# A convolution and a focused linear attention over 16 images: where the last state product, the norms, the high half of O and the floor stand, and inner loops written out

## What is computed

```python
x = x + _L0_conv_ref(_gn(x), ...)   # 3x3 grouped convolution, 8 groups of 32; kernels rotated by an
                                    # angle that a small MLP finds per image; output scaled per channel
x = x + _L1_conv_ref(_gn(x), ...)   # focused linear attention, 8 heads of 32:
#   q, k = relu(x Wq + bq) + 1e-6, relu(x Wk + bk) + 1e-6, both divided by softplus(scale)
#   q = q**3 * |q| / |q**3| ; k likewise            (norms over all 256 channels of a token)
#   z = 1 / (q . sum_tokens(k) + 1e-6) ; state = sum_tokens(k^T v) ; out = (q @ state) * z
#   out = out + depthwise 5x5 convolution of v ;  out = out @ Wproj + bproj
```

## Time and profile before

| | before |
|---|---|
| median of 3 runs (lowest to highest) | 3786.84 us (3786.37 to 3790.71) |
| the profiled execution: its own time | 3783.43 us |
| its span | 3781.6 us |
| PE busy, share of the span | 3485.4 us, 92% |
| DVE, ACT, POOL busy | 73%, 70%, 42% |
| mean granted TensorE clock | 0.989 |

### The profile page before, as it was taken

One profiled execution on the slowest core, in us unless ns is written; L12 is line 12 of the kernel. 1 busy time (PEld: TensorE's weight loads), 2 busy tenths in 40 slices (PEclk: granted clock), 3 DMA queues, 4 the chain that ended last, 5 costly groups with the idle time before them and its releaser, 6 DMA issues.

```text
span 3781.6 us, 84370 instructions
## 1 busy us (share of the span) xinstructions
PE 3485.4 (92%) x27988; PEld 2840.5 (75%) x27988; DVE 2762.7 (73%) x6715; ACT 2658.7 (70%) x7096; POOL 1606.0 (42%) x1557
## 2 busy tenths in 40 slices
PE   1669999999999999999999999999999999999897
PEld 1238787877878778787877878787787878778786
DVE  7776876767787676777767677776767777575747
ACT  2347777777777777777867777776777777676775
POOL 5542553625345262544626254462625436250402
PEclk9889999999999999999999999999999999999999
DMA  6662634536354453635445363544626343360402
GB/s 222 207 194 68 188 114 143 156 108 190 104 171 118 142 170 97 192 113 161 122 141 176 92 191 120 150 130 124 196 80 192 118 148 113 109 181 1 119 6 79
DMA packets 559906, 515.10 MB, mean 136 GB/s; under 512 B 97600, under 2 KB 491968, under 8 KB 559552
## 3 DMA queue, kind: packets, MB, share of 16 engines
q1 hardware_dynamic: 555200, 508.99, 44.7%
q10 hardware_dynamic: 4352, 1.57, 0.2%
HBM read 351.06 MB, written 134.22 MB: 128 GB/s over the span
## 4 chain that ended last, share of the span: by engine, by line
PE 76%; DVE 10%; ACT 8%; issue 4%; DMA 1%; SPq 1%; POOL 0%; DVEq 0%; ACTq 0%; POOLq 0%
PE SM L1524 15%; PE F L1541 15%; PE VAB L1541 8%; PE PP L1632 7%; PE F L1580 6%; PE VAB L1580 6%; PE T L1552 5%; PE VAB L1610 5%; PE T L1601 3%; PE F L1543 2%; ACT K L1308 2%; PE T L1620 2%; PE VAB L1543 1%; DVE F L996 1%; DVE XR L1068 1%
## 5 line engine op out<-in xcount | busy, mean ns | idle before, releaser
L1541 PE MATMUL F<-WQ,XHL 128*128 128x256 f16 x6144 | 812.7, 273 | 15.9 <-ACT V L1345 15.9
L661 POOL TENSOR_TENSOR XR<-XR,V 128x512 f32<-128x512 f32 x256 | 325.8, 1273 | 904.3 <-DVE XR L1057 904.3
L1314 ACT ACTIVATE K<-K,SCAL 128x256 f32<-128x256 f32 x1024 | 514.0, 509 | 225.4 <-DVE K L1002 224.6
L636 POOL TENSOR_TENSOR SL<-PL,SL 128x1122 f16<-128x1122 f32 x112 | 259.9, 2320 | 970.5 <-DVE SL L970 970.5
L1541 PEld LDWEIGHTS F<-WQ,XHL 128*128 128x128 f16 (+1 forms) x6144 | 599.9, 98 | 89.6 <-issue 19.8
L1524 PE MATMUL SM<-SL,BD 128*128 128x512 f16 x2688 | 634.9, 385 | 0.0
L1308 ACT ACTIVATE K<-F,SCAL 128x256 f32<-128x256 f32 x1024 | 474.8, 469 | 215.3 <-DVE F L996 213.3
L1002 DVE TENSOR_TENSOR K<-K,F 128x512 f32<-128x512 f32 x512 | 350.4, 684 | 228.8 <-PE T L1552 112.3
L1524 PEld LDWEIGHTS SM<-SL,BD 128*128 128x128 f16 x2688 | 260.9, 97 | 284.2
L996 DVE TENSOR_TENSOR F<-F,FL 128x512 f32<-128x512 f32 x512 | 353.5, 690 | 144.5 <-PE F L1543 139.5
L1632 PE MATMUL PP<-XR,WP 128*128 128x256 f16 x3072 | 380.6, 274 | 46.1 <-DVE XR L1075 46.1
(11 more groups left out here) (202 smaller groups left out, 6864.1 us busy)
## 6 DMA issues: line engine op xcount, KB each, us to landing
XR<-xr SPq DMA_DIRECT2D x132, 512.0 KB, 5.0
U<-x SPq DMA_DIRECT2D x256, 256.0 KB, 3.4
XR<-x SPq DMA_DIRECT2D x256, 256.0 KB, 4.1
out<-XR SPq DMA_DIRECT2D x256, 256.0 KB, 3.4
PL<-xp SPq DMA_DIRECT2D x112, 561.0 KB, 3.8
RX<-xr SPq DMA_DIRECT2D x118, 512.0 KB, 3.8
x<-RX SPq DMA_DIRECT2D x448, 128.0 KB, 2.8
BD<-RX SPq DMA_DIRECT2D x240, 96.0 KB, 2.2
```

The lines of the kernel that those rows point to most:

```text
L661: g_.tensor_tensor(o, o, fm, ALU.add).then_inc(o_rdy, 2)
L1314: a.activation(K2[:, p, t * C:(t + 1) * C], K3[:, p, t * C:(t + 1) * C], ACT.Square, scale=inv_a, accum_out=S6[:, 2 * p + t:2 * p + t + 1] ...
L1541: t_.matmul(o, XHL[:, xa, h, at], WQ[:, wa, h, c0:c0 + C], start=(k == 0), stop=False)
```

## The change

- The last pair's `accumulate_state` and the closing matmuls move behind channel 1 of the depthwise convolution (`last_state`). On DVE `low_v` of the last pair goes ahead of `ratio` and `scale_k` of it. The small matmuls between channels and ACT's `root` move back by two channels.
- PE no longer waits for all evictions before the first query projection, but for channels 0 to 28 before the first and for all before the second.
- On ACT `high_out` stands ahead of `attn_input` in a query step. Where there is no convolution (the last two batches) `squares` stands ahead of `norms`, and on DVE `floor_max` ahead of `ratio` and `low_out`.
- The loops `Fori` of `step_kv` are Python loops on all three engines.
- Every `carry` is gone.

```diff
-        def carry(eng):
-            eng.sem_inc(carried, 1)
...
@@ DVE, step_q
+                if not conv and (live(p) or keys):
+                    floor_max(n, p)
                 if conv and 0 <= k < 2 * GROUPS:
                     result_stats(b + 2, k)
...
-                if live(p) or keys:
+                if conv and (live(p) or keys):
                     floor_max(n, p)
@@ DVE, batch
-                with dve.Fori(1, 5) as u:
+                for u in range(1, 5):
...
+                low_v(b, NU - 1, 1)
                 ratio(n, 1, S2, S6)
                 scale_k(n, 1)
-                low_v(b, NU - 1, 1)
@@ ACT, depthwise
-                    if ahead >= 1 and c == 21:
+                    if ahead >= 1 and c == 23:
                         root(b + 4)
@@ ACT, step_q
+                if live(p - 3):
+                    high_out(b, u - 2 + p, 1 - p)
                 if nxt:
                     attn_input(b + 1, u - 3, p)
-                if live(p - 3):
-                    high_out(b, u - 2 + p, 1 - p)
...
                 if live(p - 1):
                     transposed_q(b, u - 1 + p, 1 - p)
+                if not conv and (live(p) or keys):
+                    squares(n, p)
+                if live(p - 1):
                     norms(n - 1, 1 - p, den_eps)
                 elif keys and p == 1:
                     norms(n - 1, 1 - p, inv_a2)
-                if live(p) or keys:
+                if conv and (live(p) or keys):
                     squares(n, p)
@@ ACT, batch
-                with act.Fori(1, NU) as u:
+                for u in range(1, NU):
@@ PE
+            def last_state(b):
+                accumulate_state(b, NU - 1, 1)
+                for h in range(HALVES):
+                    fin = t_.matmul(T[h][:, 0:P + 2], ONES[0:32, :], NOT[:, :], start=False, stop=True)
+                fin.then_inc(state_full, 1)
...
+                    if c == 1:
+                        last_state(b)
-                    if ahead >= 1 and c == 17:
+                    if ahead >= 1 and c == 19:
                         group_mean(b + 4)
...
                     pe.wait_ge(f_cube, b * 2 * PAIRS + PAIRS + 2 * u + p + 1)
+                    if u == 0:
+                        pe.wait_ge(fm_rdy, HD * b + (HD - 3 if p == 0 else HD) + FM_CR)
                     project(b, u, p, F, 0)
...
-                with pe.Fori(1, 5) as u:
+                for u in range(1, 5):
...
-                for p in range(2):
-                    accumulate_state(b, NU - 1, p)
-                for h in range(HALVES):
-                    fin = t_.matmul(T[h][:, 0:P + 2], ONES[0:32, :], NOT[:, :], start=False, stop=True)
-                fin.then_inc(state_full, 1)
+                accumulate_state(b, NU - 1, 0)
                 pe.wait_ge(v_lo, PAIRS * (b + 1) + VLO_CR)
                 pe.wait_ge(f_cube, b * 2 * PAIRS + PAIRS + CUBE_CR)
...
                 depthwise(b, ahead)
-                pe.wait_ge(fm_rdy, HD * (b + 1) + FM_CR)
                 pe.wait_ge(state_rdy, 4 * HPH * (b + 1))
```

More of the change, by code:

```diff
@@ L198, in conv_then_focused_attention @@
         z_rdy = sem("z_rdy")
-        carried = sem("carried")
         ready = sem("ready")
@@ L346, in load_taps @@
                     sp.wait_ge(tp_rdy, i - 2)
-                    carry(sp)
                 sp.dma_start(taps_tile(i), toeplitz[:, i * PIX:(i + 1) * PIX]).then_inc(taps_in[i % 3], 16)
@@ L573, in link @@
                 pool.wait_ge(rot_chain, c * N_ROT + steps[0])
-                carry(pool)
             def rotation(c, between=lambda j: None):
@@ L858, in deviations @@
                 dve.wait_ge(s0_rdy, pixels)
-                carry(dve)
                 if not early(k):
                     dve.wait_ge(s1_rdy, results)
-                    carry(dve)
                 for layer in range(2):
@@ L1583, in depthwise @@
                     ins.then_inc(dw_full, 1)
-                    if ahead >= 1 and c == 17:
+                    if c == 1:
+                        last_state(b)
+                    if ahead >= 1 and c == 19:
                         group_mean(b + 4)
-                    if ahead >= 1 and c == 19:
+                    if ahead >= 1 and c == 21:
                         group_spread(b + 4)
-                    if ahead >= 3 and c == 23:
+                    if ahead >= 3 and c == 25:
                         patch_mean(b + 3)
-                    if ahead >= 3 and c == 26:
+                    if ahead >= 3 and c == 28:
                         hidden(b + 3)
-                    if ahead >= 3 and c == 28:
+                    if ahead >= 3 and c == 30:
                         heads(b + 3)
@@ L1658, in step_q @@
                         pe.wait_ge(o_rdy, 2 * PAIRS * (b + 1) + O_CR)
-                        carry(pe)
                     values(b + 1, 0, p)
```

## The result

| | before | after |
|---|---|---|
| median (lowest to highest) | 3787.49 us (3786.37 to 3790.71, 4 runs) | 3852.91 us (3852.46 to 3855.85, 4 runs) |
| ratio after/before, 95% interval | | 1.0174 [1.0161, 1.0187] |
| span of the profiled execution | 3781.6 us | 3850.6 us |
| DVE busy | 2762.7 us, 73% | 2951.8 us, 77% |
| PE busy | 3485.4 us | 3508.8 us |

What follows compares the result with a forecast made beforehand. PE's busy time was taken as the floor, only its idle time to be had. 19.2 + 2.8 + 8.4 + 6.7 = 37.1 us off 3783.43 gave 3746.3; with 3.4 for the median, say 3749.5 us; range 3737 to 3767.

Steps and rivals of the forecast that it cites:

- Loops and `carry`: Inner loops written out and increments removed, on all engines: 0, at most 2 us gained in the start phase.
- The last state product: End of keys and values, all 16 batches: PE's 0.91 us wait for scaled keys goes; 1.2 us a batch, 19.2 us.
- T's waits: PE's waits for scaled keys before the last state additions: from 32 waits and 37.6 us to 16 and about 23.
- The wait for evictions: Before the first query projection: 1.0 us in batch 13, 0.9 each in 14 and 15, elsewhere nothing; 2.8 us.
- rival (a): End of the depthwise stage: both waits really fall, another 13 us, 3736; chance 0.06.
- `high_out` first: Before the last output projection: low half of O comes earlier, 0.6 us in 14 batches with a convolution; 8.4 us.
- Batches 14 and 15: Attention steps and batch 14's last output: shorter waits by floor and squares sooner; 6.7 us, bounds 2 and 9.
- Rival (d): Written-out loops make instruction fetch fall behind, so the kernel gets slower: 3822; chance 0.04.
- rival (b): TensorE's clock falls behind PE's waits; 7 us, chance 0.12; its own wording is not in the text given.
- (c): The waits come back elsewhere, at depthwise channel 0 or the norm matmuls: half the gain, 3768; chance 0.15.
- (e): All waits are refilled by the chain behind them: no effect beyond 0.2%, 3785; chance 0.04.
- the waits named as a sign of being wrong: Depthwise matmuls waiting for `low_v`, a larger patch-mean wait, or PE idle put down to "issue" in keys and values.

Runs made afterwards that it cites:

- the sixth experiment: The kernel with all increments back and all new orders, with the inner loops over units 1 to 4 as loops again on DVE, ACT and PE: 3740.3 us.
- the first three experiments: One POOL increment (conv_low) back in the kernel after: 3760.12 us; the same out of the kernel before: 3880.75; kernel after with DVE's ratio ahead of high: 3771.52.
- the fifth: The kernel after with two increments back on POOL, behind the low-half wait and behind each rotation link's wait: 3745.09 us.

## Why the prediction was wrong, point by point

**The step that failed** is "Loops and `carry`": "The increments lie beside longer waits; POOL's and SP's take nothing from PE. 0, at most 2 us gained in the start phase." For the loops it held within the 4 us that the sixth experiment leaves open. For the increments it was wrong by about 116 us: 3852.91 without them, 3736.36 with them. I priced an increment as time of its own engine, which on POOL was free, and did not ask what POOL's earlier start would meet. The row that would have warned stood in the trace of before: the `RATIO` product had a mean of 322 ns beside a usual 160, so it was held somewhere already, and in a query step with a cast it slipped in ahead of POOL by 0.08 us. No rival named this. The loss has three places: the low halves (93 us: the first three experiments), the rotation (15 us: the fifth), and 9 us more between two kernels whose intervals overlap. The traces, one of each, put 8 of these into batch 14, where the same product is held by POOL's low half of the next image's input; this was read, not tried.

How 0.6 us of wait becomes so much: PE's output projections of the kernel after lie 7.47 and 8.05 us apart in turn (882.26, 889.73, 897.78) where they lay 7.28 apart before (864.78, 872.06). That is 0.96 us for each pair of steps, of which the list of waits shows 0.60: the matmuls' modelled ends reach over and hide the first 0.1 to 0.2 us of each delay. Against the kernel with one increment a batch is 6.3 us longer (227.6 and 221.3), which is 6.5 such pairs. PE's busy time is too high for the same reason (3508.8 us, against 3467.0 with all increments, for the same matmuls).

**The new orders** can be judged on the kernel with all increments, whose change is the predicted one without the `carry` part. A batch without a fall of the clock takes 222.07 us before and 220.0 to 220.3 in it, where 1.2 + 0.6 = 1.8 us less were predicted. From the first state wait to the end it needs 50.5 us less (3450.3 and 3399.8), 10.2 of it clock. The other 40.3 stand against a predicted 37.1. The four single terms below add up to 42; from one trace each, a few us of a term are noise.

**The last state product**: 19.2 us predicted, 17.7 measured without the clock. T's waits came to 23.0 us in 16, as forecast ("about 23"). The mechanism and the size were right.

**The wait for evictions**: 2.8 predicted, 3.3 read in the last three batches; the ratios cannot tell so little from nothing. Elsewhere it moved to the transposes (1.37 us; 1.2 were predicted), so rival (a) fell.

**`high_out` first**: 8.4 predicted, 13.4 measured without the clock. In the batches with a convolution it is 0.6 to 0.9 us where 0.6 was taken; 2.12 became 1.41 to 1.42. Batch 14, for which this term had nothing, gave 2.9 more.

**Batches 14 and 15**: 6.7 predicted, 7.6 measured, inside the bounds of 2 and 9. The attention's waits were forecast at about 33 us and came to 36.6: without this order they would be 41.1 in the new kernel, not the 38.2 of before.

**Loops**: 0 predicted, nothing clear of the noise measured. Rival (d), slower by fetching, had the right side and the wrong cause: the fetch queue's 26 packets more (24 were predicted) stand also in the fastest kernel. The Trainium skill (Runtime: NRT & Kernel Launch, Instruction fetch mechanics) has a taken branch stall when its target lies out of the window that is held. No view here shows whether the turns of these short loops leave it, so the prediction's "at each turn" went further than the page; the batches with and without loops agree to 0.3 us.

**The clock, rival (b)**: given 0.12 and 7 us, it was what happened where the increments stayed. The falls of the kernel before, 10.2 us, are gone in that with all increments. The price of one fall was read too low: the working took 1.2 us from one window and 1.00 around it, but the next window, 1226 to 1230, has 0.87, so a fall costs 1.7 us and six cost 10.2. The working's sum without the clock missed that kernel, 3749.5 against 3736.4, for the most part by this. The Trainium skill (TensorE: Matmul & The Clock Gate, Part 1: The HAM clock gate), that idleness brings the throttle back, agrees with every fall lying behind a wait. What decides between two like waits stays open: the last output projection's wait of 2.12 us let the clock fall in seven batches of one kernel and in two of the kernel before, and the state's two waits in six batches of 16.

**Rivals (c) and (e)** fell: with the increments there the gain was 1.3%, and none of the waits named as a sign of being wrong came up.

## What to carry to other kernels

An instruction that does nothing but take 0.1 us on one engine can decide which of two engines is held by the other; before removing it, look at what starts within 0.2 us of it on the other engine, and at any small operation whose mean is above its minimum. Where such a race is found, settle it by an order or a dependence rather than by a delay, but measure, since the new order moves other meetings (here it cost 10 us). And where a wait of 1 to 2 us stands on PE, its price is not only its length: in this kernel the fallen clock behind such waits cost about as much again (state product, high half of O) or nothing (evictions).

## What the runs showed of the hardware

- A semaphore increment between a POOL wait and the operation behind it delays that operation's start by about 0.10 us (0.18 and 0.08 us from the releaser's end; 0.26 with two increments).
- A 128x2 DVE product of two SBUF operands takes 0.16 us alone and up to 2.31 us when POOL started 0.02 us sooner on a 2.31 us operation: it is held until that one ends. Beside a POOL operation of 1.16 us that started 0.12 us sooner it takes 1.06 us.
- Clock falls stand at one place of a kernel in some batches and not in others with the same wait before them, in one kernel mostly in every second batch (444 us apart). By the sums above one fall cost 1.7 us, at three places of one kernel 3.4.
